# Cross-attention, block attention and a ternary feed-forward: value products ahead of the next scores, one quantization per slot

## The chip, the cores and the metric

The kernel runs on one core of one Trainium2 chip. The metric is the device time of one execution in microseconds. Three runs of the kernel before took 1119.99, 1122.01 and 1123.82 us; the median is 1122.01.

## The reference

`x` is 32 batches of 64 tokens of width 512, `ctx` is 32 batches of 1601 rows of width 512 with a mask. Three residual layers follow each other:

```python
x = x + xattn(layernorm(x), ctx, mask)   # 4 query heads of 128, one key/value head, rotary positions
x = x + attn(layernorm(x))               # 16 heads of 32, causal over the 64 tokens of a batch
x = x + ffn(layernorm(x))                # 512 -> 2048 -> 512

# attn
Q, K, V = heads(x @ WQ), heads(x @ WK), heads(x @ WV)
p = softmax(Q @ K.T / sqrt(32) + causal)
out = (p @ V) @ WO

# ffn: both weight matrices are made ternary in the kernel
gamma = mean(abs(W)) + 1e-6
Wq = sign(W / gamma) * minimum(round(abs(W / gamma)), 1)
h = layernorm(gelu(x @ Wq_fc.T)) * ln_w + ln_b
out = h @ Wq_proj.T
```

## The kernel before

All of it is one program with one instruction list per engine. A function at the head of the program looks at the mask and, when few context rows are valid, takes the path `few`, which is the one that runs here. Its stages are: cross-attention over 32 batches (0 to about 541 us), block attention over 16 blocks of 128 tokens, two batches each (about 541 to 835 us), and the feed-forward over the same 16 blocks (to the end).

The order of the work is written out by hand. `at(slot, order, fn)` enters a piece of work under a slot and an order number; `run_slots` then calls the pieces slot by slot and, within one, by order number. Each piece appends its instructions to the lists of its engines, so a smaller number means an earlier place on every engine that the piece uses. Each engine works through its list in order and stops at a wait. Waits are named by tokens (`tok[...]`). Slots are places in the order and have no fixed length.

Block attention begins at slot `B2`, and block i at `s = B2 + 4*i`. Below, slots are counted from `B2`. The even and the odd block of a pair share the projections (`s2_qk`, moving operand 256 columns), so the pattern repeats every eight slots:

- `s2_T` (order 5): transposes the layer-normed input of a block; ScalarE writes the high part of the split, VectorE the low part. `s2_qk` (4.1), one of eight groups a slot, for a later pair; each is 12 products (three terms of a split times four), evacuated by ScalarE. `s2_v` (4.4): the values, 12 products of 512 columns, and four small DMAs.
- `s2_scores` (order 1): 64 small matmuls into four PSUM banks; VectorE adds the causal mask (L930) and takes the maxima (L933), GpSimd subtracts them (L936).
- `s2_exp` (slot s+1): ScalarE, two halves b. `s2_PT` (s+2 and s+3, 2.7): four transposes each, evacuated by ScalarE (L949) for the value products.
- `s2_PV` (s+4, 4): the value products, 64 small matmuls; VectorE normalizes (L971 reciprocal, L974 product). This slot is also that of the scores of block i+1.
- `s2_ET` (s+5, 5.5): transposes of the normalized values and their split: high part on ScalarE (L230), low part on VectorE (L233). `s2_O` (s+6, 4.45): the output projection, 12 products of 512 columns, and `store`: VectorE adds the residual (L861), a DMA stores the rows.

Beside this run the 64 tiles of the feed-forward weights. `w_load(n)` loads tile n into one of four buffers; it is issued when tile n-4 is done with. For n below 32 `w_abs(n)` (3.9) sums absolute values on VectorE (L1008). Then `w_gamma` makes the scale: a small sum (L1015), one matmul with ones (L1018, the scale product), two small VectorE instructions. For n from 32, `w_quant(n)` (4.5) makes a ternary tile with two VectorE instructions (L1035, L1038) in one of two buffers, so it waits for the transposes of tile n-2. `w_T(n)` transposes it on TensorE (L1050, four bf16 matmuls, "ternary transposes" below), and ScalarE evacuates (L1059). In the kernel before `w_quant(n)` first calls `w_T(n - 1)`. Slots: tiles are spread evenly over 62 slots, from slot 1 to slot 62.

At the end of the stage the ternary weights are copied to float (`s3_WF`, L1125 on ScalarE, L1128 on VectorE, two each; slot 62, order 7.4, which waits for everything emitted until then), and the first feed-forward products `s3_h(0, n)` stand at slot 64 and following, order 1.5. The evacuation of the last block's second `s2_PT` (slot 63) stands behind these copies on ScalarE.

PSUM banks come from one list: a piece takes the bank that was given back longest ago.

Of the kernel before, what the change touches and what calls it, by code (L numbers as in the profile page):

```python
# [160 lines left out]
def few(nc, handle, bank, base, x1d, x2d, x, ctxd, mask, rms, qw, kvw, ow, WQ, WK, WV, WO, Wfc, lnw, lnb,  # L161
        Wproj, cosk, sink, cosq, sinq, identd, causald, out, picked, kmask, ktab, t_rows, nb=B):
    ni = nb // 2
# [237 lines left out]
    def at(slot, order, fn):  # L401
        count[0] += 1
        sched.setdefault(slot, []).append((order, count[0], fn))
# [273 lines left out]
    for b in range(nb):  # L677
# [22 lines left out]
        else:  # L700
            i = b // 2
# [20 lines left out]
    T0, B2 = FT * nb + 2, FT * nb + 24  # L722
# [216 lines left out]
    def s2_exp(i, b):  # L939
        tok["exp", i, b] = [op("act", lambda e: e.activation(  # L940
            sP[:, b, :, :], sP[:, b, :, :], ACT.Exp, scale=float(DK) ** -0.5), sem("a_exp"), [tok["nm", i, b]])]
# [11 lines left out]
    def s2_PV(i):  # L953

        ks = take(), take()
        free = [t for k in ks for t in gfree[k]]
        for b in range(2):
            for c in range(4):
                for x in range(2):
                    ps = slice(64 * x, 64 * x + 64)  # L960
                    for s in range(2):
                        m = (b * 4 + c) * 33
                        tk = products(bank[ks[x]][64 * s:64 * s + 64, m:m + 33],
                                      [(PT2[ps, b, c * 128 + 64 * s:c * 128 + 64 * s + 64],
                                        Vb[ps, i % 2, b, c, s, :])],
                                      "a_pv", [*tok["pt", i, 0], *tok["pt", i, 1], *tok["v", i], *free], check=True)
        tok["pv", i] = [tk]
        en = en2[:, :].rearrange("p (c b x f) -> p x b c f", c=4, b=2, x=2)
        for x in range(2):
            src = bank[ks[x]][:, 0:264].rearrange("p (b c f) -> p b c f", b=2, c=4)  # L970
            tr = op("dve", lambda e, x=x, src=src: e.reciprocal(rc2[:, x, :, :], src[:, :, :, 32]), sem("a_rc"),  # L971
                    [tk, *d2("en", i - 1)])
            rc = rc2[:, x, :, :].unsqueeze(3).to_broadcast([128, 2, 4, 32])
            t = op("dve", lambda e, x=x, src=src, rc=rc: e.tensor_tensor(en[:, x, :, :, :], src[:, :, :, 0:32], rc, ALU.mult),  # L974
                   sem("a_en"), [tr, *tok["late"], *d2("enT", i - 1)])
            give(ks[x], [t])
        tok["en", i] = [t]

    def s2_ET(i):
        k = take()  # L980
        dst = bank[k][:, :].rearrange("p (c r) -> p c r", c=4)
        tt = transposes(dst, [en2[:, c * 128:(c + 1) * 128] for c in range(4)], "a_enT",
                        [*tok["en", i], *gfree[k]])
        tok["enT", i] = [tt]
        tok["ET", i] = split("a_ET", dst, ET2[0][:, :, :], ET2[1][:, :, :], [tt, *tok["late"], *d2("o2", i - 1)])
        give(k, tok["ET", i])

    def s2_O(i):
        k = take()
        terms = []  # L990
        for c in range(4):
            terms += three(ET2[0][:, c, :], ET2[1][:, c, :], Wh[3][:, c, :], Wl[3][:, c, :])
        tk = products(bank[k][:, :], terms, "a_o", [*tW[3], *tok["ET", i], *gfree[k]])
        tok["o2", i] = [tk]
        store(i, x2d, k, tk)
# [11 lines left out]
    def w_abs(n):  # L1007
        ta = op("dve", lambda e: e.tensor_reduce(  # L1008
            asum[:, n // 16, n % 16:n % 16 + 1], wn[:, n % 4, :], AX.X, ALU.add,
            apply_absolute_value=True), sem("f_as"), [t_wn[n]])  # L1010
        wfree[n] = [ta]
        w_load(n + 4)
# [14 lines left out]
    def w_quant(n):  # L1027

        if n == 32:
            w_gamma()  # L1030
        else:
            w_T(n - 1)
        m = (n - 32) // 16
        w = wq_[:, n % 2, :]
        tq = op("dve", lambda e: e.tensor_scalar(w, wn[:, n % 4, :], gam[:, m:m + 1], -1.0,  # L1035
                                                 ALU.is_gt, ALU.add),
                sem("f_q"), [t_wn[n], *tok["gam"], *tok["late"], *tok.get(("wT", n - 2), [])])
        tq = op("dve", lambda e: e.scalar_tensor_tensor(  # L1038
            w, wn[:, n % 4, :], gam[:, 2 + m:3 + m], w, ALU.is_ge, ALU.add), sem("f_q"), [tq])
        wfree[n] = [tq]  # L1040
        if n + 4 < 64:
            w_load(n + 4)
        tok["wq", n] = [tq]

    def w_T(n):
        m, t = divmod(n - 32, 16)
        k = take()
        dst = bank[k][:, 0:256].bitcast(BF).rearrange("p (c r) -> p c r", c=4)
        for c in range(4):
            tt = op("pe", lambda e, c=c: e.transpose(dst[:, c, :], wq_[:, n % 2, c * 128:(c + 1) * 128],  # L1050
                                                     identb[:, :]),
                    sem("f_wT") if c == 3 else None,
                    [*tok["wq", n], t_idb, *gfree[k]] if c == 0 else ())
        tok["wT", n] = [tt]
        if m == 0:
            o = WFb[:, :, t * 128:(t + 1) * 128]
        else:
            o = WPb[:, (t % 4) * 4:(t % 4) * 4 + 4, (t // 4) * 128:(t // 4) * 128 + 128]
        tok["wb", m] = [op("act", lambda e: e.activation(o, dst, ACT.Copy), sem("f_W"),  # L1059
                           [tt, *tok["late"]])]  # L1060
        give(k, tok["wb", m])

    for i in range(ni):
        s, u, v = B2 + 4 * i, i // 2, i % 2
        o = B2 + 8 * u - 14 + 2 * v if u > 1 else (T0 - 7 + 2 * v if u == 0 else T0 + 4 + 2 * v)
        at(o - 1, 0, lambda i=i: ln_load(i))
        at(o, 3.4, lambda i=i: ln_stats(i))
        at(o + (1 if u > 1 else 3), 4.3, lambda i=i: ln_apply(i))
        at(B2 + 8 * u - 11 + v if u > 1 else T0 + 10 * u, 5, lambda i=i: s2_T(i))
        at(s - 1 if u else T0 + 10 + v, 4.4, lambda i=i: s2_v(i))  # L1070
        at(s, 1, lambda i=i: s2_scores(i))
        for b in range(2):
            at(s + 1, 3.0 + b, lambda i=i, b=b: s2_exp(i, b))
            at(s + 2 + b, 2.7, lambda i=i, b=b: s2_PT(i, b))
        at(s + 4, 4, lambda i=i: s2_PV(i))
        at(s + 4, 0, lambda i=i: res_load(i))
        at(s + 5, 5.5, lambda i=i: s2_ET(i))
        at(s + 6 if i else s + 8, 4.45, lambda i=i: s2_O(i))
    for u in range(ni // 2):
        for c in range(8):  # L1080
            at(B2 + 8 * u - 9 + c if u > 1 else T0 + 2 + c + 10 * u, 4.1 if u > 1 else 0.7,
# [15 lines left out]
    at(B2 + 3, 8.7, s2_outs)  # L1097
    at(B2 + 3, 8.8, lambda: s2_wload(3))
    for n in range(64):
        s = B2 - 2 + (n * (4 * ni - 2)) // 64  # L1100
        if n < 4:
            at(B2 - 1, 0.5, lambda n=n: w_load(n))
        if n < 32:
            at(s + 3, 3.9, lambda n=n: w_abs(n))
        else:
            at(s + 3, 4.5, lambda n=n: w_quant(n))
    B3 = B2 + 4 * ni
    at(B3 - 1, 9, lambda: w_T(63))

# [1269 lines left out]
```

How the kernel before makes its waits and increments, by code:

```python
    def op(self, eng, fn, sem=None, waits=(), inc=1):  # L47
        for w in waits:
            if w is None:
                continue
            s, v = w
            if self.seen[eng].get(s, 0) < v:
                self.seen[eng][s] = v
                self.q[eng].append(lambda e, s=s, v=v: e.wait_ge(s.h, v))
        if sem is None:
            self.q[eng].append(fn)
            return None
        self.q[eng].append(lambda e: fn(e).then_inc(sem.h, inc))
        sem.n += inc
        return (sem, sem.n)
# [7 lines left out]
        def f(e):  # L68
            with e.If(when()):
                for g in fns[:-1]:
                    g(e)
                fns[-1](e).then_inc(sem.h, 1)
            with e.Else():
                e.drain().then_inc(sem.h, 1)
# [267 lines left out]
        def g(e):  # L342
            with e.If(when()):
                f(e).then_inc(s.h, 16)
            with e.Else():
                e.sem_inc(s.h, 16)
# [1956 lines left out]
        def run(name, e):  # L2303
            early.play(name, e)
            first.play(name, e)
            fits = e.value_load(onepath[0:1, 0:1], min_val=0, max_val=1)
            with e.If(fits > 0):
                short.play(name, e)
            with e.Else():
                for s, n in [rows, *loaded[1]]:
                    e.wait_ge(s.h, n)
                long.play(name, e)
```

## Time and profile before

| what | value |
|---|---|
| median of three runs | 1122.01 us |
| profiled execution | 1122.38 us |
| its span | 1120.2 us |
| mean granted TensorE clock | 0.969 of full speed |
| TensorE busy | 956.8 us (85%) |
| VectorE busy | 688.4 us (61%) |
| ScalarE busy | 453.0 us (40%) |
| GpSimd busy | 441.0 us (39%) |
| mean of one L861, L1008, L1015 | 0.69, 0.67, 0.18 us |
| weight tile load, issue to landing (median) | 3.0 to 3.2 us |

TensorE busy times are modelled and overlap at the edges; a stop of TensorE is better read from the order of time, where a bracket gives the idle time in front of a group and the instruction that ended it. VectorE and ScalarE are half idle on the whole; what they do matters where TensorE stops for it. The granted clock has two levels, 1.2 and 2.4 GHz, shown as 0.5 and 1.0.

### The profile page before, as it was taken

How to read it: one execution, taken by the hardware profiler on the slowest of the kernel's cores; microseconds unless marked ns; L12 is line 12 of the kernel's file. 1: busy time of each engine (PE TensorE's matmuls, PEld its weight loads, DVE VectorE, ACT ScalarE, POOL GpSimd, SP SyncE). 2: the span in 40 equal slices, each digit the busy share in tenths (PEclk: the TensorE clock that was granted, in tenths of full speed). 3: DMA queues.
4: the chain of work that ended last, by engine and by line, in shares of the span. 5: the costliest groups of instructions: out<-in, count | busy, mean ns of one | idle time of the engine just before them, and what ended most of it. 6: DMA issues, size and time to landing. Idle time of an engine off the chain costs nothing.

```text
span 1120.2 us, 22904 instructions
## 1 busy us (share of the span) xinstructions
PE 956.8 (85%) x7466; PEld 809.4 (72%) x7466; DVE 688.4 (61%) x1352; ACT 453.0 (40%) x972; POOL 441.0 (39%) x572
## 2 busy tenths in 40 slices
PE   0898879888788888779798988889869999999996
PEld 0787757676676767668688887778647888888885
DVE  3587666766766767764545554655556665565554
ACT  2565445554455545444323232434363322322321
POOL 1354444444444444410212111111016767667663
PEclk9999999999999999979799998999879999999999
DMA  5532233221223222411534443334331111101101
GB/s 167 156 92 55 71 89 95 89 60 59 84 83 92 72 80 73 158 38 40 170 116 112 114 136 95 107 108 108 107 118 38 58 34 52 57 29 57 57 19 50
DMA packets 96769, 95.11 MB, mean 85 GB/s; under 512 B 41634, under 2 KB 58099, under 8 KB 96371
## 3 DMA queue, kind: packets, MB, share of 16 engines
q1 hardware_dynamic: 96016, 93.19, 28.3%
q8 instruction: 74, 1.21, 0.4%
q14 instruction: 69, 0.56, 0.2%
q10 hardware_dynamic: 578, 0.13, 0.1%
q0 software_dynamic: 32, 0.02, 0.0%
HBM read 76.45 MB, written 12.66 MB: 80 GB/s over the span
## 4 chain that ended last, share of the span: by engine, by line
PE 66%; DVE 15%; issue 10%; ACT 3%; DVEq 2%; ACTq 1%; POOL 1%; DMA 1%; SPq 0%; POOLq 0%
PE bank L244 52%; PE bank L219 9%; PE bank L240 4%; DVE f L233 3%; DVE f L507 2%; DVE f L930 2%; DVEq L74 1%; ACT f L230 1%; ACTq L74 1%; ACT f L412 1%; PE bank L529 1%; DVE f L974 1%; DVE f L470 1%; DMA f<-in_L_attn_WO_dram 1%; DVE f L641 1%
## 5 line engine op out<-in xcount | busy, mean ns | idle before, releaser
L244 PE MATMUL bank<-f,f 128*128 128x512 f32 (+3 forms) x5544 | 762.0, 312 | 62.4 <-issue 24.5
L244 PEld LDWEIGHTS bank<-f,f 128*128 128x128 f32 (+2 forms) x5544 | 596.5, 173 | 165.9 <-issue 67.6
L233 DVE TENSOR_TENSOR f<-bank,f 128x512 fp32r<-128x512 f32 x291 | 194.4, 686 | 129.9 <-ACT f L230 127.9
L219 PE MATMUL bank<-f,f 128*128 128x128 f32 x1152 | 170.3, 282 | 62.9 <-DVE f L619 28.7
L230 ACT ACTIVATE f<-bank 128x512 fp32r<-128x512 f32 x291 | 167.1, 593 | 110.3 <-PE bank L219 105.5
L219 PEld LDWEIGHTS bank<-f,f 128*128 128x128 f32 x1152 | 136.8, 145 | 90.1 <-DVE f L619 29.8
L936 POOL TENSOR_TENSOR f<-f,f 128x512 f32<-128x512 f32 x32 | 33.4, 1043 | 219.0 <-DVE f L933 219.0
L1153 ACT ACTIVATE f<-bank 128x512 f32<-128x512 f32 x64 | 38.3, 599 | 175.5 <-PE bank L244 175.5
L1176 POOL TENSOR_TENSOR f<-f,f 128x512 f32<-128x512 f32 x62 | 79.7, 1285 | 67.4 <-DVE f L1172 67.4
L468 POOL TENSOR_TENSOR f<-f,f 128x512 f32<-128x512 f32 x32 | 41.9, 1310 | 156.6 <-ACTq L74 135.2
L1178 POOL TENSOR_TENSOR f<-f,f 128x512 f32<-128x512 f32 x62 | 80.5, 1299 | 4.9
L261 POOL TENSOR_SCALAR f<-f 128x1 f32<-128x1 f32 (+1 forms) x112 | 22.9, 204 | 151.3 <-DVE f L840 84.5
L263 POOL TENSOR_TENSOR f<-f,f 128x1 f32<-128x1 f32 (+1 forms) x112 | 78.0, 697 | 9.3
L930 DVE TENSOR_TENSOR f<-bank,f 128x256 f32<-128x256 f32 x64 | 24.0, 418 | 72.5 <-PE bank L244 72.5
L518 ACT ACTIVATE f<-f,f 128x512 f32<-128x512 f32 x64 | 46.3, 724 | 50.4 <-DVE f L516 40.5
L884 ACT ACTIVATE f<-bank 128x256 f32<-128x256 f32 x64 | 24.4, 381 | 89.6 <-PE bank L244 89.6
L507 DVE CUSTOM_DVE_ANT_0 f<-bank,f 128x512 f32<-128x512 f32 x64 | 44.2, 690 | 25.3 <-PE bank L244 17.7
L240 PE MATMUL bank<-f,f 128*128 128x256 f32 x372 | 53.1, 290 | 7.5 <-issue 4.7
L240 PEld LDWEIGHTS bank<-f,f 128*128 128x128 f32 x372 | 46.6, 190 | 13.5 <-issue 13.3
L230 ACT ACTIVATE f<-f 128x256 fp32r<-128x256 f32 (+1 forms) x52 | 25.3, 497 | 70.8 <-DVE f L565 68.9
L861 DVE TENSOR_TENSOR f<-bank,f 128x512 f32<-128x512 f32 x32 | 22.1, 691 | 44.3 <-PE bank L244 44.3
L1172 DVE TENSOR_SCALAR f<-f,f,f 128x512 f32<-128x512 f32 x64 | 37.1, 580 | 16.4 <-POOL f L263 16.4
(88 smaller groups left out, 819.0 us busy)
## 6 DMA issues: line engine op xcount, KB each, us to landing
f<-in_ctx_dram SPq DMA_DIRECT2D x71, 256.0 KB, 2.8
f<-x_scratch SPq DMA_DIRECT2D x64, 256.0 KB, 3.0
f<-in_x_dram SPq DMA_DIRECT2D x32, 256.0 KB, 3.0
x_scratch<-f SPq DMA_DIRECT2D x32, 256.0 KB, 2.0
f<-in_L_ffn_W_fc_dram SPq DMA_DIRECT2D x32, 256.0 KB, 3.0
f<-in_L_ffn_W_proj_dram SPq DMA_DIRECT2D x32, 256.0 KB, 3.2
f<-in_ktab_dram SPq DMA_DIRECT2D x71, 64.0 KB, 2.0
f<-f SPq DMA_DIRECT2D x64, 64.0 KB, 2.4
```

The source lines that it names most:

```text
L219: f = lambda e, i=i, a=a: e.transpose(dst[:, i, :], a, ident[0:rows, 0:rows])
L230: return maybe("act", lambda e: e.activation(hi, src, ACT.Copy), sem(name + "_hi"), waits, when)
L233: return maybe("dve", lambda e: e.tensor_tensor(lo, src, hi.bitcast(F32), ALU.subtract), sem(name + "_lo"), waits, when)
L240: fns = [lambda e, i=i, a=a, b=b: e.matmul(dst, a, b, start=(first and i == 0), stop=(last and i == n - 1), skip_group_check=True) for i, ...
L244: f = lambda e, i=i, a=a, b=b: e.matmul(dst, a, b, start=(first and i == 0), stop=(last and i == n - 1), skip_group_check=check)
L263: return op("pool", lambda e: e.tensor_tensor(dst, tmp, mhalf[0:dst.shape[0], 0:n], ALU.pow), sem(name + "_p"), [t])
L468: ta = op("pool", lambda e: e.tensor_tensor(o1, K, cb, ALU.mult), sem("s_k1"), [tk, t_tab[b], *d("ktT", b - 2)])
L507: to = op("dve", lambda e: e.tensor_tensor_reduce(Pm[:, b % 2, t, :], bank[NL][:, :], bias[:, b % 2, :], 1.0, -3.0e38, ALU.add, ALU.max, m ...
L518: te = op("act", lambda e: e.activation(Pm[:, u, t, :], Pm[:, u, t, :], ACT.Exp, bias=nm[:, u, t:t + 1], accum_out=den[:, u, t:t + 1]), se ...
L930: f = lambda e, src=src, o=to[:, x, :, :]: e.tensor_tensor(o, src, cb, ALU.add)
L1176: t2 = op(eng, lambda e: e.tensor_tensor(g, g, lw[:, sl], ALU.mult), sem(f"f_y_{eng}"), [t1, tok["ln"]])
L1178: tok["y", i, n] = op(eng, lambda e: e.tensor_tensor(g, g, lb[:, sl], ALU.add), sem(f"f_y_{eng}"), [t2])
```

## The change

The value products of block i stand ahead of the scores of block i+1 in the same slot (order 0.5 instead of 4). Their output transposes stand at the end of that slot instead of the next (s+4, 5.5), and the output projection at the end of the slot after it (s+5, 5.6) instead of in slot s+6. The second half of the exponential stands at order 4.6 instead of 4.0. The absolute sums are spread over slots 1 to 26; quantization n follows with one tile a slot, in slots 27 to 58, at the beginning of its slot (0.3); `w_T(n)` is no longer called by `w_quant` but stands at order 4.5 of the slot after its quantization (28 to 59). No instruction is added or taken away.

```diff
@@ -1028,8 +1028,6 @@
 
         if n == 32:
             w_gamma()
-        else:
-            w_T(n - 1)
         m = (n - 32) // 16
         w = wq_[:, n % 2, :]
         tq = op("dve", lambda e: e.tensor_scalar(w, wn[:, n % 4, :], gam[:, m:m + 1], -1.0,
@@ -1070,12 +1068,12 @@
         at(s - 1 if u else T0 + 10 + v, 4.4, lambda i=i: s2_v(i))
         at(s, 1, lambda i=i: s2_scores(i))
         for b in range(2):
-            at(s + 1, 3.0 + b, lambda i=i, b=b: s2_exp(i, b))
+            at(s + 1, 3.0 + 1.6 * b, lambda i=i, b=b: s2_exp(i, b))
             at(s + 2 + b, 2.7, lambda i=i, b=b: s2_PT(i, b))
-        at(s + 4, 4, lambda i=i: s2_PV(i))
+        at(s + 4, 0.5, lambda i=i: s2_PV(i))
         at(s + 4, 0, lambda i=i: res_load(i))
-        at(s + 5, 5.5, lambda i=i: s2_ET(i))
-        at(s + 6 if i else s + 8, 4.45, lambda i=i: s2_O(i))
+        at(s + 4, 5.5, lambda i=i: s2_ET(i))
+        at(s + 5 if i else s + 7, 5.6, lambda i=i: s2_O(i))
     for u in range(ni // 2):
         for c in range(8):
             at(B2 + 8 * u - 9 + c if u > 1 else T0 + 2 + c + 10 * u, 4.1 if u > 1 else 0.7,
@@ -1097,15 +1095,15 @@
     at(B2 + 3, 8.7, s2_outs)
     at(B2 + 3, 8.8, lambda: s2_wload(3))
     for n in range(64):
-        s = B2 - 2 + (n * (4 * ni - 2)) // 64
+        s = B2 - 2 + (n * (4 * ni - 38) // 32 if n < 32 else 4 * ni - 70 + n)
         if n < 4:
             at(B2 - 1, 0.5, lambda n=n: w_load(n))
         if n < 32:
-            at(s + 3, 3.9, lambda n=n: w_abs(n))
+            at(s + 3, 0.3, lambda n=n: w_abs(n))
         else:
-            at(s + 3, 4.5, lambda n=n: w_quant(n))
+            at(s + 3, 0.3, lambda n=n: w_quant(n))
+            at(s + 4, 4.5, lambda n=n: w_T(n))
     B3 = B2 + 4 * ni
-    at(B3 - 1, 9, lambda: w_T(63))
```

## Rows read from the trace of the kernel before

**Rows 1.** Chain of waits of the whole execution, share of the span by engine.

```profile
PE 66%; DVE 15%; issue 10%; ACT 3%; DVEq 2%; ACTq 1%; POOL 1%; DMA 1%; SPq 0%; POOLq 0%
```

**Rows 2.** TensorE's waits from 540 to 840 us: total, times, longest.

```profile
PE bank L1050 <- DVE f L1038: 17.4, 9, 4.0
...
PE bank L244 <- DVE f L233: 8.8, 6, 2.2
...
PE bank L219 <- DVE f L974: 7.0, 6, 2.8
```

**Rows 3.** TensorE in order of time (start, length), part that quantizes; idle time in brackets.

```profile
714.04 4.41 PE L244 MATMUL bank<-f,f 128*128 128x256 f32 x24 [1.54 <-DVE f L233]
...
718.62 4.25 PE L244 MATMUL bank<-f,f 32*64 32x64 f32 x140
...
725.54 0.40 PE L1050 MATMUL bank<-f,f 128*128 128x128 bf16 x4 [0.95 <-DVE f L1038]
...
743.82 0.40 PE L1050 MATMUL bank<-f,f 128*128 128x128 bf16 x4 [1.75 <-DVE f L1038]
...
757.05 4.25 PE L244 MATMUL bank<-f,f 32*64 32x64 f32 x140
...
787.39 2.98 PE L244 MATMUL bank<-f,f 128*128 128x512 f32 x12
...
790.22 0.40 PE L1050 MATMUL bank<-f,f 128*128 128x128 bf16 x4
```

**Rows 4.** TensorE, part that only sums: two pair starts, and waits of 580 to 620.

```profile
616.35 10.06 PE L244 MATMUL bank<-f,f 128*128 128x256 f32 x176
...
651.45 8.74 PE L244 MATMUL bank<-f,f 128*128 128x256 f32 x165
...
PE bank L219 <- DVE f L974: 1.6, 2, 1.0
...
PE bank L244 <- DVE f L233: 1.2, 1, 1.2
```

**Rows 5.** TensorE in order of time, last two blocks and start of stage 3.

```profile
790.55 2.63 PE L244 MATMUL bank<-f,f 32*64 32x64 f32 x128
...
797.47 0.61 PE L1050 MATMUL bank<-f,f 128*128 128x128 bf16 x4 [3.96 <-DVE f L1038]
...
800.39 4.95 PE L244 MATMUL bank<-f,f 128*128 128x512 f32 x12 [0.61 <-issue]
...
808.95 2.63 PE L244 MATMUL bank<-f,f 32*64 32x64 f32 x128
...
830.37 7.43 PE L244 MATMUL bank<-f,f 128*128 128x512 f32 x80 [3.95 <-DVE f L1128]
```

**Rows 6.** VectorE in order of time behind one block's scores.

```profile
699.34 0.76 DVE L930 TENSOR_TENSOR f<-bank,f 128x256 f32<-128x256 f32 x2 [3.16 <-PE bank L244]
...
702.12 0.68 DVE L839 BATCH_NORM_STATS2 f<-f 128x6 f32<-128x512 f32 x1
...
702.94 0.19 DVE L971 RECIPROCAL f<-bank 128x8 f32<-128x8 f32 x1
...
704.07 0.48 DVE L1035 TENSOR_SCALAR f<-f,f 128x512 bf16<-128x512 f32 x1
```

**Rows 7.** TensorE around the scale product.

```profile
674.70 4.06 PEld L244 LDWEIGHTS bank<-f,f 32*64 32x64 f32 x140 [0.35 <-issue]
...
683.12 2.91 PE L244 MATMUL bank<-f,f 128*128 128x256 f32 x12
```

**Rows 8.** Window of one microsecond: busy time of PE, PEld, DVE, ACT, POOL; granted clock.

```profile
794.00:795.00 1.00, 0.00 (x0) 0.00 (x0) 0.97 (x3) 0.39 (x2) 0.82 (x1) 0.68 0.41 65
```

**Rows 9.** TensorE and ScalarE in the first pair.

```profile
548.84 3.46 PE L244 MATMUL bank<-f,f 32*64 32x64 f32 x128
...
548.95 0.60 ACT L949 ACTIVATE f<-bank 128x512 f32<-128x512 f32 x1 [0.72 <-PE bank L219]
...
561.59 14.37 PE L244 MATMUL bank<-f,f 128*128 128x256 f32 x188 [2.20 <-DVE f L233]
```

## The prediction

> **What bounds the kernel now.** I read the chain of waits first [rows 1]: TensorE carries two thirds of it, so the time falls only where TensorE stops. The change touches the second stage alone (541 to 835 us). There the list of TensorE's waits [rows 2] names what stops it: the ternary transposes waiting for the quantization (17.4 us), the next projection waiting for the low part of its input (8.8) and the output transposes waiting for the normalized values (7.0). Then I went through TensorE's order of time. One block of 128 tokens is four slots, two blocks share a projection; call slot 0 the first slot of stage 2. In the part that quantizes [rows 3] a pair of blocks takes 38.4 us (718.62 to 757.05), and three stops recur in it: 1.75, 0.95 and 1.54, together 4.25. In the part that only sums absolute values [rows 4] it takes 35.1 (616.35 to 651.45), with stops of 1.6 in two and 1.2, together 2.8. Without stops a pair costs 32.3, or 34.2 with eight ternary transposes.
>
> **The change part by part.** No instruction is added or removed; the sum is over stops, and over places where the clock falls.
>
> *Work per piece.* Score products take 1.25 us and value products as much (2.63 for both at full clock [rows 5]), a 512-column group 2.8 (787.39, next work at 790.22 [rows 3]), a projection group 1.5, four transposes 0.4, four ternary ones 0.25. On VectorE [rows 6] the mask additions and maxima of one block run from 699.34 to 702.12, 2.8; statistics to 702.94, 0.8; normalization to 704.07, 1.15; one quantization 1.2. Masks start 0.5 after the last score product.
>
> *Quantization and its transposes.* Quantization n now stands at the head of a slot, its transposes near the end of the next. It waits for the transposes of n-2 (the slot before, TensorE's last item there), so it starts about 0.15 into the slot and ends at 1.35. Behind it on VectorE is the normalization, which cannot start before the value products end (1.25) plus 0.5 = 1.75. So it hides, with 0.4 to spare, and a whole slot later nothing waits for it: the stops of 1.75 and 0.95 go. If that cover were gone, each such block pays up to 1.2 - 0.4 = 0.8.
>
> *Value products ahead of the scores.* The normalization then runs 1.75 to 2.9, beside the scores (1.25 to 2.5); masks follow at 3.0 (0.5 after the scores), where they would have started anyway. The output transposes come after scores, one projection group and the ternary transposes, at 4.3: no stop, so the 1.6 go too.
>
> *Output projection a slot sooner.* This costs. Its input's low part is a VectorE subtraction emitted at the end of the slot of the scores, behind masks (3.0 to 5.8) and, in every second block, the statistics (to 6.6). With 0.65 for itself and 0.15 to be seen, the projection can start at 6.6 or 7.4. TensorE arrives at 4.3 + 0.4 + 1.5 + 0.25 = 6.45 (6.8 with one input transpose between): stops of 0.15 and 0.6; without ternary transposes it is there 0.5 sooner, so 0.65 and 1.1. Before, a slot more hid this. The stop of the next projection stays, 1.54 falling to 1.2 (its subtraction no longer stands behind a quantization).
>
> Per pair: 34.2 + 0.15 + 0.6 + 1.2 = 36.15 with quantization, against 38.4: -2.3. Without it 32.3 + 0.65 + 1.1 + 1.2 = 35.2, against 35.1: +0.1.
>
> *Stretch by stretch.* Slots 8 to 24: two pairs, +0.2. Slots 24 to 32: four of the ternary transposes move in here (+1.1), stops 0.65 + 0.6 + 1.15 for 2.8 (-0.4), and the scale's product, now at slot 27. It follows on VectorE the output addition (0.7), the last sum (0.65), statistics (0.8) and a small sum (0.2), seen 2.8 after the projection's end, while TensorE arrives after 0.4 + 1.5: 1.0 and its own 0.3. Together +2.0. Slots 32 to 40: before, the pair with the scale product took 718.62 - 674.70 = 43.9, as TensorE stood before it and after it, then ran at half clock, 1.2 of 2.4 GHz (2.91 for 12 matmuls of 256 columns [rows 7]); I take 43.7, since the first mark is a weight load. Now an ordinary 36.1: -7.6. Slots 40 to 48: -2.3. Slots 48 to 56 (33.5; no input transposes or statistics): 2 x 0.95 go, 2 x 0.15 come, -1.6.
>
> *Slots 56 to 60, no projections left* [rows 5]. Before: 808.95 - 790.55 = 18.4, with a stop of 3.96 and a half-clock output projection of 4.95. Now: values and scores to 2.5, ternary 2.8, output transposes at 3.05 (normalization) to 3.45, ternary to 3.7; then the projection waits for masks (5.8), its subtraction (6.45): start 6.65, a stop of 3.0. Does the clock fall in it? It fell at 794.4 (a mean of 0.68 from 794 to 795 is 0.36 us at full clock [rows 8]), less than 1 us after TensorE's last work, and not in stops of 1.75 [rows 3]. 3.0 is nearer to 3.96 than to 1.75; I take the fall: 4.8 for the projection, to 11.45, then 0.4 + 0.25 + 0.4 + 2.85 + 0.25 to 15.6. -2.8 (warm -4.8; both ends kept).
>
> *From slot 60 to the third stage.* Before: 21.4 from 808.95 to the first product of stage 3 at 830.37, which waited for a weight conversion, itself behind the store of the projection before. Now the projection (behind masks, statistics, subtraction) starts at 7.45 and is cold, ends 12.4; three sets of transposes to 14.6; store and semaphores let the conversions on ScalarE start at 16 to 17 (2.65 after the store's issue, as before), two take 3.7, and only then comes the evacuation that the value products need, as these now stand ahead of the first product of stage 3: 20.6 to 21.7. They run 1.7 cold, then the product 3.4 cold: 25.7 to 26.8 for work that ended before at 26.6. -0.4, between -2 and +2. What leaves these slots (the four last quantizations) gains nothing more, since the chain store, conversion, evacuation ends last.
>
> *The start, slots 0 to 8* [rows 9]. Now the first value products wait for the copy of the second set of transposes (548.95 + 0.60, seen at 549.7), 0.85 after TensorE is free, and the scores behind them come 1.7 late at half clock (3.46 for both). Masks shift by 2.75, less 1.15 for the normalization now ahead of them; the input's subtraction, which holds the first projection at 561.59, lies behind all that: +1.6, a little less by ScalarE. I take +1.5, between -0.5 and +3.
>
> The exponential's new place (behind one more projection copy) costs nothing: its transposes are a slot and a half away. Weight loads are issued four sums or quantizations ahead, three slots at least, some 13 us (35.1 / 8 x 3 [rows 4]) before use, and land in about 3: nothing. Store and residual load move with the projection; the residual lands before the addition in every stretch. Bounds of all these: 0 to +1.
>
> Sum: 1.5 + 0.2 + 2.0 - 7.6 - 2.3 - 1.6 - 2.8 - 0.4 = -11.0. The profiled execution took 1122.38 (span 1120.2 and 2.2 around it), 0.4 above the median of the three runs (1122.01). 1122.4 - 11.0 = **1111.4 us**.
>
> **The rivals.** *A, the forecast.* 55%, own range 1107 to 1117.
>
> *B, the low part is no stop and the clock holds.* If VectorE reaches the subtraction before TensorE gets to the projection, the stops that I charge go: 2 x 1.75 in slots 8 to 24, 1.25 in 24 to 32, 2 x 0.75, 0.3: 6.5; and a clock that holds in slots 56 to 60 gives 2.0 more. 1109.4 with the clock alone, 1103 with both. For it: the merged VectorE rows hide overlaps of up to 0.1 per instruction. Against: the order of emission is plain. 22%. On the clock, the Trainium skill (TensorE: Matmul & The Clock Gate, What's actually happening) lets the monitor run on its own time and not from the program's start, so equal gaps may end differently; the fall after a short stand [rows 8] agrees. By that rule 1109.4 would be about as likely as 1111.4.
>
> *C, the quantization holds up the normalization.* It starts only when TensorE has done the transposes of n-2; if that is seen 0.4 later than I reckon, normalization, masks and subtraction slip in the nine blocks of slots 28 to 60, by up to 0.8: +7.5, 1118.9, no change. For it: the wait was a slot away before and is now next door. Against: 0.4 of room. 14%.
>
> *D, slower: the stop at the output projection lets the clock fall.* Place: slot 5 of each pair. If masks and subtraction come 0.9 later than reckoned, the stop of 1.1 becomes 2.0, and TensorE falls to half clock as after the scale product, where a projection group took 2.91 for 1.5 [rows 7]. Price: 0.9 x 14 blocks = 12.6, and two such groups, 2.8, in each of the three pairs of slots 8 to 32: 8.4. 1111.4 + 21 = 1132. Without a fall the delay alone must reach (11.0 + 3.4) / 14 = 1.0 per block to end slower. For it: the stop is new and recurs, and a second one of 1.2 follows some 5 us later. Against: stops of 1.75 recur without a fall [rows 3]. 9%.
>
> **How the numbers follow.** About 0.3% (3.4 us) is what a measurement of this kernel can tell from no change. A and B are faster: 0.77; C is same: 0.14; D slower: 0.09. The range takes in most of B and C: 1103 to 1120.
>
> **What would show it.** Right: waits of the ternary transposes for the quantization near zero, no wait of output transposes for the normalization, a pair with quantization near 36.1, the scale product costing 1 to 1.5 with no half clock behind it; and a new wait of TensorE for the split's subtraction just ahead of the output projection, 0.15 to 1.1, then 3 in slot 57 and 4 in slot 61. Wrong: ternary transposes still waiting (C), granted clock under 1.0 in slots 8 to 56 (D), or a first product of stage 3 that starts as late after slot 60 as before while its value products are still to come.

## The result and the profile after

The changed kernel takes **1112.41 us** (median of 5 runs, 1107.35 to 1112.48) against 1122.01 of the kernel before: a ratio of 0.990, interval 0.987 to 0.993. Forecast were 1111.4 and "faster".

The stretches are read from the starts of the value evacuations (L900), one in each block, from the first score product (541.45 us before, 544.18 after), and from the first full group of 16 products of stage 3 (856.62 before, 846.61 after).

| slots | before | after | difference | forecast |
|---|---|---|---|---|
| 0 to 8 | 26.1 | 27.1 | +0.95 | +1.5 |
| 8 to 24 | 72.1 | 72.1 | 0.0 | +0.2 |
| 24 to 32 | 35.1 | 35.9 | +0.8 | +2.0 |
| 32 to 40 | 43.7 | 35.9 | -7.8 | -7.6 |
| 40 to 48 | 38.4 | 35.7 | -2.7 | -2.3 |
| 48 to 56 | 33.5 | 31.6 | -1.9 | -1.6 |
| 56 to 60 | 18.4 | 15.2 | -3.2 | -2.8 |
| 60 to stage 3 | 47.8 | 48.9 | +1.1 | -0.4 |
| rest | 263.6 | 263.6 | 0.0 | 0 |
| first score product to end | 578.7 | 566.0 | **-12.7** | -11.0 |

Below, "first score to end" is this last row, for every kernel, from its profiled execution. It ends with a piece that no edit touches, from the last addition to the end of the span, 6.96 to 8.39 us in the twelve kernels; differences of about 1 us can lie there alone. The span shrank by only 10.0: stage 1, which is the same code, was 2.7 longer in this execution. TensorE's busy time and mean granted clock between 150 and 165 us, first after, then before (columns: window, its length, PE busy, clock, DMA share, GB/s):

```profile
150.00:165.00 15.00, 12.25 (x58) 0.81 0.39 124
```

```profile
150.00:165.00 15.00, 11.92 (x69) 1.00 0.44 132
```

The clock fell there in one execution and not in the other. So the forecast's total is nearer to the median (1.0) than its stage-2 sum is to the measured one (1.7), and that is luck.

TensorE's waits in stage 2 after (total, times, longest), to be set beside [rows 2]:

```profile
PE bank L244 <- DVE f L233: 11.5, 10, 2.8
PE bank L244 <- ACT f L949: 8.1, 2, 7.4
PE bank L244 <- issue: 6.3, 6, 3.8
...
PE bank L1018 <- DVE f L1015: 0.4, 1, 0.4
PE bank L219 <- DVE f L974: 0.3, 1, 0.3
```

The ternary transposes (17.4 before) are gone from the list, the normalization (7.0) nearly so. New are the waits of the output projection for the low part of its input, part of L233 and all of "issue" (in each of the six places the subtraction ends 0.1 before the projection starts), and 7.4 of the last value products behind L949. The chain of waits [rows 1] breaks off after a quarter of the span, at a load in stage 3 that GpSimd waits for; that load comes up again below.

TensorE in order of time after, the part that only sums [rows 4]:

```profile
580.57 3.04 PE L244 MATMUL bank<-f,f 128*128 128x512 f32 x12 [0.49 <-DVE f L233]
...
597.40 3.04 PE L244 MATMUL bank<-f,f 128*128 128x512 f32 x12 [0.79 <-issue]
...
604.26 8.61 PE L244 MATMUL bank<-f,f 128*128 128x256 f32 x164 [1.07 <-DVE f L233]
...
615.23 3.04 PE L244 MATMUL bank<-f,f 128*128 128x512 f32 x12 [0.49 <-DVE f L233]
```

The 512-column groups are the output projections: stops of 0.49 and 0.79 (forecast 0.65 and 1.1), then 1.07 for the next pair's input. A pair takes 34.66 (580.57 to 615.23; forecast 35.2, before 35.10). The pair in front of it, which still holds the start of the stage, takes 37.5 for 37.0, so slots 8 to 24 come out even. The part that quantizes [rows 3]:

```profile
703.26 3.03 PE L244 MATMUL bank<-f,f 128*128 128x512 f32 x12 [0.33 <-issue]
...
710.69 4.42 PE L244 MATMUL bank<-f,f 128*128 128x256 f32 x24 [1.41 <-DVE f L233]
...
715.28 4.25 PE L244 MATMUL bank<-f,f 64*64 64x33 f32 x140
...
751.01 4.25 PE L244 MATMUL bank<-f,f 64*64 64x33 f32 x140
```

A pair takes 35.73 (715.28 to 751.01; forecast 36.15, before 38.4), with 0.33 and 1.41 left of 4.25. VectorE at the head of a slot with scores [rows 6]:

```profile
715.98 0.75 DVE L1036 SCALAR_TENSOR_TENSOR f<-f,f,f 128x512 bf16<-128x512 f32 x1
716.93 0.21 DVE L971 RECIPROCAL f<-bank 128x8 f32<-128x8 f32 x1 [0.20 <-PE bank L244]
```

The normalization waits 0.20 for the value products, not for the quantization ahead of it. The scale product now stops TensorE for 0.4, and the projection behind it runs at full clock, where [rows 7] show 2.91 for 12 matmuls (here 24 in 4.42):

```profile
655.18 0.38 PE L1018 MATMUL bank<-f,f 128*128 128x2 f32 x2 [0.41 <-DVE f L1015]
...
655.81 4.42 PE L244 MATMUL bank<-f,f 128*128 128x256 f32 x24
```

The last two blocks [rows 5], TensorE and then ScalarE:

```profile
782.63 2.64 PE L244 MATMUL bank<-f,f 64*64 64x33 f32 x128
...
789.25 4.30 PE L244 MATMUL bank<-f,f 128*128 128x512 f32 x12 [2.79 <-DVE f L233]
...
797.85 2.64 PE L244 MATMUL bank<-f,f 64*64 64x33 f32 x128
...
805.21 5.46 PE L244 MATMUL bank<-f,f 128*128 128x512 f32 x12 [3.76 <-issue]
...
819.65 5.46 PE L244 MATMUL bank<-f,f 64*64 64x33 f32 x72 [7.40 <-ACT f L949]
```

```profile
815.35 3.71 ACT L1123 ACTIVATE f<-f 128x2048 fp32r<-128x2048 bf16 x2 [2.85 <-DMA f<-x_scratch]
818.97 0.58 ACT L949 ACTIVATE f<-bank 128x512 f32<-128x512 f32 x1
```

Stops of 2.79 and 3.76 (forecast 3 and about 4). Then the two conversions, 3.71, with the evacuation of the probabilities behind them, and TensorE idle 7.40 for it. The clock in slot 57 (columns: window, its length, busy time of PE, PEld, DVE, ACT, POOL, clock, DMA share, GB/s):

```profile
790.00:791.00 1.00, 1.00 (x5) 0.78 (x4) 0.70 (x1) 0.29 (x1) 0.00 (x0) 0.81 0.00 0
791.00:792.00 1.00, 1.00 (x3) 0.79 (x3) 0.00 (x0) 0.00 (x0) 0.00 (x0) 0.50 0.00 0
```

It fell at about 790.6 (0.81 of that microsecond), more than 1 us after TensorE was at work again, and was back at 794.

### The profile page after: what moved, and what is told of

Same layout as the page of the kernel before. It is cut to its first block and busy times, and to the rows that moved or that the text cites. A ratio compares the mean times of both kernels' runs of the same rounds, so it can differ in the third digit from the quotient of the medians.

```text
span 1110.2 us, 22910 instructions
## 1 busy us (share of the span) xinstructions
PE 956.3 (86%) x7466; PEld 809.7 (73%) x7466; DVE 693.2 (62%) x1352; ACT 452.8 (41%) x972; POOL 443.4 (40%) x572
## 5 line engine op out<-in xcount | busy, mean ns | idle before, releaser
L233 DVE TENSOR_TENSOR f<-bank,f 128x512 fp32r<-128x512 f32 x291 | 194.5, 685 | 128.8 <-ACT f L230 126.8
L230 ACT ACTIVATE f<-bank 128x512 fp32r<-128x512 f32 x291 | 167.4, 593 | 112.7 <-PE bank L219 107.5
L263 POOL TENSOR_TENSOR f<-f,f 128x1 f32<-128x1 f32 (+1 forms) x112 | 79.8, 713 | 9.3
L507 DVE CUSTOM_DVE_ANT_0 f<-bank,f 128x512 f32<-128x512 f32 x64 | 44.2, 690 | 25.7 <-PE bank L244 18.4
L230 ACT ACTIVATE f<-f 128x256 fp32r<-128x256 f32 (+1 forms) x52 | 25.3, 496 | 69.4 <-DVE f L565 69.0
L412 ACT ACTIVATE f<-f 128x512 bf16<-128x512 f32 x71 | 44.0, 620 | 3.2 <-ACT f L412 2.2
```

What stands on the lines that cost most here:

```text
L230: return maybe("act", lambda e: e.activation(hi, src, ACT.Copy), sem(name + "_hi"), waits, when)
L233: return maybe("dve", lambda e: e.tensor_tensor(lo, src, hi.bitcast(F32), ALU.subtract), sem(name + "_lo"), waits, when)
L263: return op("pool", lambda e: e.tensor_tensor(dst, tmp, mhalf[0:dst.shape[0], 0:n], ALU.pow), sem(name + "_p"), [t])
L412: done["sq"] = maybe("act", lambda e: e.activation(sq[:, :], cx[:, b % NG, t, :], ACT.Square, accum_out=ss[:, b % 4, t:t + 1]), sem("s_ss" ...
L507: to = op("dve", lambda e: e.tensor_tensor_reduce(Pm[:, b % 2, t, :], bank[NL][:, :], bias[:, b % 2, :], 1.0, -3.0e38, ALU.add, ALU.max, m ...
```

## The experiments

Experiments 1 to 4, 5 to 8, and 9 and 10 ran on one chip each, beside the kernel before.

### 1. The weights' half of the change alone

The kernel after with the attention's lines as before, all edits on sums, quantizations and ternary transposes kept:

```
-            at(s + 1, 3.0 + 1.6 * b, lambda i=i, b=b: s2_exp(i, b))
+            at(s + 1, 3.0 + b, lambda i=i, b=b: s2_exp(i, b))
...
-        at(s + 4, 0.5, lambda i=i: s2_PV(i))
+        at(s + 4, 4, lambda i=i: s2_PV(i))
-        at(s + 4, 5.5, lambda i=i: s2_ET(i))
-        at(s + 5 if i else s + 7, 5.6, lambda i=i: s2_O(i))
+        at(s + 5, 5.5, lambda i=i: s2_ET(i))
+        at(s + 6 if i else s + 8, 4.45, lambda i=i: s2_O(i))
```

> Only the weight part of the change: absolute sums in slots 1 to 26, one quantization at the head of a slot, transposes a slot later; value products, output transposes, output projection and exponential stand as before. Measured from the first score product of stage 2 to the end of the span: 578.7 us before, 566.0 with the whole change. Theory (the gain is the weight part's: scale product and its half clock, ternary transposes that no longer wait; moving the attention pieces brings stops of its own): about 560, 556 to 564, so more gain than the whole change; no wait of TensorE for the quantization, waits of the output transposes for the normalization of 0.4 at most, none of the output projection for the subtraction. Rival (the value products ahead of the scores bring the gain): 572 to 577.

Measured: 1105.39 us (1103.84 to 1106.52), 0.984 of before (0.982 to 0.987); first score to end 563.6, 2.4 below the whole change. Slots 32 to 40 take 35.8, as after. That is 3.6 above the theory's 560 and far from the rival: all of the gain, and more, comes from the weights' half. Of the theory's signs, no ternary transpose waits for its quantization. The output projection does wait for the subtraction, 0.35 in three places, and the normalization stops TensorE for 0.41 in the part that sums but for 2.2 to 3.1 in the first pair and the last two blocks. Slots 8 to 24 take 70.3 for 72.1 with no edit on the attention: there only the place of the sums differs.

### 2. The attention's half alone

The kernel before with those lines of the kernel after.

> Only the attention part: value products ahead of the next scores, output transposes and projection sooner, second exponential later; the weights are summed, quantized and transposed in their old places. First score product to the end: theory 577 to 583 (no gain: the scale product keeps its stop and half clock, the ternary transposes still wait, now for a quantization behind masks, and the output projection waits for a subtraction behind that quantization); rival 566 to 572.

Measured: 1133.22 us (1130.2 to 1136.19), 1.009 of before (1.006 to 1.013); first score to end 589.7. Neither theory went so far up. TensorE in the part that sums:

```profile
578.63 3.04 PE L244 MATMUL bank<-f,f 128*128 128x512 f32 x12 [1.09 <-DVE f L233]
...
596.05 3.04 PE L244 MATMUL bank<-f,f 128*128 128x512 f32 x12 [1.38 <-issue]
```

The same two stops as after, each 0.6 longer: the sums stand in their old place (3.9), one of them (0.7 on VectorE) ahead of the subtraction that the projection needs. That is 2.3 of the loss of 11.0, in slots 8 to 24. Slots 48 to 56 lose 3.4 and the way to stage 3 3.0. In slot 49 the clock falls at the output projection, and 20 us later, behind stops of the same length (1.40 before the ternary transposes, then 0.25), it does not:

```profile
769.96 4.58 PE L244 MATMUL bank<-f,f 128*128 128x512 f32 x12 [0.25 <-issue]
...
789.85 3.04 PE L244 MATMUL bank<-f,f 128*128 128x512 f32 x12 [0.25 <-issue]
```

### 3. The change with the output projection in its old slot

```
-        at(s + 5 if i else s + 7, 5.6, lambda i=i: s2_O(i))
+        at(s + 6 if i else s + 8, 4.45, lambda i=i: s2_O(i))
```

> The whole change, but the output projection back in its old place (a slot later). First score product to the end, 566.0 with the change: theory 562 (the stops of 0.5, 0.8 and 0.3 ahead of the projections in slots 8 to 56 go, 4 us in all, and no stop takes their place; the last blocks are about even). Rival (the earlier projection pays at the end of the stage, where its store is waited for): 567 to 570.

Measured: 1102.31 us (1101.69 to 1105.31), 0.982 of before (0.979 to 0.985); first score to end 559.3. TensorE in the part that sums has no stop at the output projections, and those of the normalization (L974) stay away too:

```profile
599.41 8.62 PE L244 MATMUL bank<-f,f 128*128 128x256 f32 x164 [1.07 <-DVE f L233]
...
610.09 0.66 PE L219 MATMUL bank<-f,f 128*128 128x128 f32 x4 [0.20 <-ACT f L940]
```

That is 2.7 better than the theory. Slots 8 to 24 take 69.0 (72.1 after). The sooner output projection costs 6.7 us (7.7 up to the last addition); the other attention moves gain 4.3 (563.6 to 559.3; 3.9 up to the last addition). In the change the one ate up the other.

### 4. The weight conversions for stage 3 a slot sooner

They wait for the last value projection alone and stand in the third slot from the end:

```
-    at(B3 - 2, 7, lambda: mark("qkv_end"))
+    at(B3 - 3, 5.2, lambda: tok.update(qkv_end=tok["proj", ni // 2 - 1]))
     for n in range(4):
-        at(B3 - 2, 7.4, lambda n=n: s3_WF(n))
+        at(B3 - 3, 5.3, lambda n=n: s3_WF(n))
```

> The whole change, and the copies of the first feed-forward weights to float a slot earlier and waiting only for the last value projection, whose weights they overwrite, not for everything emitted (the store of a projection among it). First score product to the end, 566.0 with the change: theory 557.5 (the stop of 7.4 ahead of the last value products falls to about 1, and TensorE's clock does not fall in it, some 2 us more). Rival (the copies on VectorE and ScalarE now delay the split of the last blocks, and the time is given back ahead of the output projection): 562 to 565.

Measured: 1106.68 us (1104.04 to 1108.16), 0.985 of before (0.982 to 0.988); first score to end 564.7, the rival's number. From slot 60 to stage 3 it takes 46.5 for 48.9; the last piece behind the last addition is 0.9 longer here. TensorE at the last value products, then ScalarE a little later:

```profile
810.29 3.28 PE L244 MATMUL bank<-f,f 64*64 64x33 f32 x72 [0.84 <-ACT f L949]
...
818.24 6.41 PE L244 MATMUL bank<-f,f 128*128 128x512 f32 x20 [2.38 <-DVE f L233]
```

```profile
814.99 1.28 ACT L1151 ACT_TABLE_LOAD   x1 [3.00 <-issue]
...
816.78 0.59 ACT L230 ACTIVATE f<-bank 128x512 fp32r<-128x512 f32 x1
```

The stop of 7.40 is down to 0.84. But the last split (L230) now stands behind the first activation of stage 3 and its table load, and TensorE waits 2.38 there, still at half clock. A wait taken away, and the next one met.

### 5. The sums and the scale product sooner, nothing else

The kernel before with the sums in slots 1 to 26 and the scale product in slot 27:

```
...
-        s = B2 - 2 + (n * (4 * ni - 2)) // 64
+        s = B2 - 2 + (n * (4 * ni - 38) // 32 if n < 32 else (n * (4 * ni - 2)) // 64)
...
+    at(B2 + 27, 0.3, w_gamma)
```

> The kernel before, with one part of the change alone: the absolute sums in slots 1 to 26 and the scale product in slot 27; quantization, transposes and attention stay where they were. Measured from the first score product to the end of the span (578.8 us before, 566.0 after, 563.6 with all edits on the weights). Theory: the 7.8 us that slots 32 to 40 lost come from the scale product leaving a place where TensorE stood 1.6 us before it and then ran at half clock; slots 32 to 40 take 38.4 like slots 40 to 48 before, slots 24 to 32 1 more: 573 to 576. Rival: the stop and the half clock go along with the product, and the gain was the quantization's: 577 to 580.

Measured: 1123.77 us (1119.87 to 1127.21), 1.001 of before (0.999 to 1.003); first score to end 578.8. The theory fails: slots 32 to 40 take 41.2, only 2.5 less. The total is the rival's, its reason is not: slots 24 to 32 take 35.9, as after, so the stop and the half clock did not go along with the product. TensorE in slots 32 to 40:

```profile
684.80 0.61 PE L1048 MATMUL bank<-f,f 128*128 128x128 bf16 x4 [2.67 <-DVE f L1036]
685.16 2.83 PE L244 MATMUL bank<-f,f 128*128 128x256 f32 x12
```

The scale product no longer stands there, but the first ternary transposes still wait for their quantization, 2.67, and behind them 12 matmuls take 2.83 again: half clock.

### 6. The quantizations at the head of their slot, nothing else

The kernel before with this (transposes where they were; the two first tiles unchanged):

```
...
-            at(s + 3, 4.5, lambda n=n: w_quant(n))
+            at(s + 3, 0.3 if n > 33 else 4.5, lambda n=n: w_quant(n))
+            if n > 32:
+                at(s + 3, 4.5, lambda n=n: w_T(n - 1))
```

> The kernel before, with another part alone: the quantizations from n = 34 at the head of their slot (0.3) and not at 4.5; the transposes stay where they are, and so do the sums, the scale product and the attention. Theory: the head of the slot is what takes away the stop of the ternary transposes (17.4 us in nine before); slots 40 to 48 35.8 (38.4 before), 48 to 56 31.6 (33.5), 56 to 60 17.5 (18.4), slot 60 to the third stage 2 less, and a part of it in slots 32 to 40: first score product to end 567 to 571 (578.8 before). Rival: a quantization at the head holds up masks and normalization as long as the value products stand behind the scores, so that the stop only moves to the output transposes: 575 to 579.

Measured: 1115.16 us (1113.71 to 1118.49), 0.994 of before (0.992 to 0.995); first score to end 573.6. Slots 40 to 48 take 35.8, 48 to 56 31.6, 56 to 60 17.1: as the theory says. Slots 32 to 40 lose 1.6 only, and the way to stage 3 does not shrink (48.4 for 47.8). The rival has a share in the last two blocks: there the output transposes wait 2.55 each for the normalization. Where the scale product stands, TensorE shows:

```profile
677.78 0.38 PE L1018 MATMUL bank<-f,f 128*128 128x2 f32 x2 [1.57 <-DVE f L1015]
...
680.00 0.61 PE L1048 MATMUL bank<-f,f 128*128 128x128 bf16 x4 [1.84 <-DVE f L1036]
680.37 2.91 PE L244 MATMUL bank<-f,f 128*128 128x256 f32 x12
```

So slots 32 to 40 lose 2.5 by one part, 1.6 by the other and 7.9 by both (experiment 1). Experiment 5 keeps a stop of 2.67, experiment 6 two of 1.57 and 1.84 close together, and in both the clock falls; in experiment 1, with neither, it is 1.00 throughout these slots.

### 7. The ternary transposes in the slot of their quantization

```
-            at(s + 4, 4.5, lambda n=n: w_T(n))
+            at(s + 3, 4.5, lambda n=n: w_T(n))
```

> The changed kernel, with the ternary transposes at the end of the slot of their quantization (slots 27 to 58), not of the next. Theory: from its head a quantization is done 1.4 us into the slot and TensorE comes to the transposes some 4 us into it, so nothing waits; the slot between is not needed: first score product to end 565 to 567 (566.0 after). Rival: the quantization waits for the transposes of tile n-2 and stands behind other VectorE work, so that the transposes wait again by 1 us or more in each of 32 slots: over 575.

Measured: 1130.41 us (1128.0 to 1133.31), 1.006 of before (1.004 to 1.008); first score to end 586.0. The rival holds, though not in each of the 32 slots: nine of the ternary transposes wait, 19.6 us in all, nearly all of them right behind a slot with scores. TensorE, and VectorE in the same slots:

```profile
709.76 0.40 PE L1048 MATMUL bank<-f,f 128*128 128x128 bf16 x4 [2.15 <-DVE f L1036]
...
710.61 4.36 PE L244 MATMUL bank<-f,f 128*128 128x512 f32 x12
```

```profile
704.27 0.76 DVE L930 TENSOR_TENSOR f<-bank,f 128x256 f32<-128x256 f32 x2
...
707.86 0.66 DVE L233 TENSOR_TENSOR f<-bank,f 128x512 fp32r<-128x512 f32 x1
708.44 0.48 DVE L1033 TENSOR_SCALAR f<-f,f 128x512 bf16<-128x512 f32 x1
708.95 0.75 DVE L1036 SCALAR_TENSOR_TENSOR f<-f,f,f 128x512 bf16<-128x512 f32 x1
```

This quantization heads its slot in the program, but VectorE still has the masks, statistics and subtraction of the slot before, 704.27 to 708.4. TensorE, which had begun the slot at 705.9, arrives at the transposes at 707.6. Where the slot before held scores and statistics, the head of a slot on VectorE comes 2.5 us into it.

### 8. Three edits to the change

Experiments 3 and 4 together, and the value projection of each even block ahead of the next pair's first key projection:

```
-        at(s - 1 if u else T0 + 10 + v, 4.4, lambda i=i: s2_v(i))
+        at(s - 1 if u else T0 + 10 + v, 4.4 if v or not u else 4.05, lambda i=i: s2_v(i))
```

> The changed kernel with three edits: the output projection back in its old slot (559.3 from the first score product to the end, when done alone), the weight conversions for the third stage released a slot sooner (564.7 alone, 1.3 less than after), and the value projection of each even block ahead of the first key projection of the next pair in the same slot, so that the low part of the input has one projection (2.8 us) more time. Theory: the stop of 1.07 before the key projection goes, six times, 1.2 more with the quantizations: 559.3 - 1.3 - 6.5 = 551.5, 549 to 554. Rival: the stop only moves (to the scores behind, or to the input transposes that come later on ScalarE): 556 to 560.

Measured: **1092.21 us** (1090.15 to 1093.6), 0.972 of before (0.969 to 0.975); first score to end 549.5, inside the theory's range. TensorE's waits in stage 2 (four of under 1 left out):

```profile
PE bank L219 <- DVE f L846: 12.3, 4, 4.9
PE bank L219 <- ACT f L940: 8.5, 6, 3.7
PE bank L244 <- ACT f L949: 1.5, 2, 0.7
```

The subtraction (L233; 11.5 after) stops TensorE nowhere. Experiment 3 still had these stops at the key projection (7.0 in six), so the third edit takes them; it was not run alone. Nearly all that is left lies in the first pair and behind slot 56.

### 9. The first block's value products behind the scores again

An edit of experiment 8's kernel:

```
-        at(s + 4, 0.5, lambda i=i: s2_PV(i))
+        at(s + 4, 0.5 if i else 4, lambda i=i: s2_PV(i))
```

> The kernel with three edits (549.5 us from the first score product to the end), and the value products of the very first block behind the scores again, as in the kernel before; all others stay ahead. Theory: the first value products stand 3.7 us behind the copy of the probabilities and hold up the scores behind them, which is the loss of 0.95 that slots 0 to 8 show; without it those slots are 1 shorter (22.5 for 23.5 in this arrangement), the total 548 to 549. Rival: the start is held by VectorE and ScalarE behind the first scores in either order, and nothing changes: 549.2 to 550.

Measured: 1089.87 us (1088.47 to 1096.17), 0.973 of before there (0.969 to 0.978), with experiment 8's interval inside it: no difference. First score to end is 548.7, which is the theory's number, but not from its place: slots 0 to 8 take 23.5 in both. TensorE:

```profile
545.60 3.46 PE L244 MATMUL bank<-f,f 32*64 32x64 f32 x128
552.28 1.97 PE L219 MATMUL bank<-f,f 128*128 128x128 f32 x8 [3.22 <-DVE f L974]
```

Scores and value products start sooner (7.4 after the first score product for 8.2), and then TensorE stands 3.22 for the normalization. The rival holds, in this arrangement. What costs slots 0 to 8 their 0.95 in the change is one of the attention's moves other than the output projection: experiment 1 without them is 0.4 under the kernel before there, experiments 2, 3 and 10 are 0.8 to 1.3 over it. Which one is left open.

### 10. The attention's half without the output projection

The kernel before with the value products, the exponential and the output transposes moved, the output projection not.

> The kernel before with the attention's moves, except the output projection, which stays in its old slot; sums, quantizations and transposes in their old places. With the output projection moved as well, this took 589.7 us from the first score product to the end (578.8 before). Theory: only the output projection's move costs (stops of 1.09 and 1.38 in each pair, for 0.99 and 0.64 that go), the others gain with any arrangement of the weights: slots 8 to 24 69 to 70 (72.1 before, 74.5 with the projection moved), the total 570 to 575. Rival: with the quantizations in their old place every attention move lengthens VectorE's queue ahead of the transposes, and the loss stays: 583 to 588.

Measured: 1121.58 us (1118.2 to 1124.0), 1.000 of before (0.998 to 1.002); first score to end 576.5, between the two. Slots 8 to 24 take 68.9, as the theory says. In the part that quantizes the rival has a share: 40 to 48 and 48 to 56 take 0.4 and 1.0 more than before, and the ternary transposes wait more, not less (17.4 before):

```profile
PE bank L1050 <- DVE f L1038: 19.5, 9, 4.2
```

## Why the prediction was right, and where not

**Quantization and its transposes: right in size, wrong in one reason.** The stops of 1.75 and 0.95 went, and the pair came to 35.7 (forecast 36.15). But the step has it start "about 0.15 into the slot" and end at 1.35. That holds in the slots with scores (679.39 to 679.57). In the slots right behind them it starts 1.7 or 2.5 into the slot (684.08 to 685.78, 700.58 to 703.07), and without a slot between, the transposes wait again (experiment 7). So the head of the slot is not enough; the slot between is needed too. The kernel before had that, with the quantization at 4.5, and it was not enough either. With sums and scale product left alone the new place brings 5.2 (experiment 6).

**Slots 32 to 40: the size right, the cause half right.** The step goes from 43.7 to an ordinary pair of 36.1. That is 5.3 for the scale product and its half clock (43.7 to 38.4) and 2.3 for the quantization. Alone the one brings 2.5 there, and nothing over the whole stage (experiment 5), the other 1.6 (experiment 6): each leaves stops behind which the clock falls. The forecast came out since the change removes both.

**Value products ahead, output projection sooner: right.** The stops at the output projection were 0.49 and 0.79 for 0.65 and 1.1, and 0 and 0.33 for 0.15 and 0.6. VectorE was as reckoned: the subtractions ended 6.47 and 7.27 after the value products of their blocks began (679.39 to 685.86, 695.89 to 703.16) for 6.45 and 7.25; TensorE came up to 0.24 later than the 6.45 and 6.8 put down. The smaller stops make a pair that only sums 0.5 shorter than forecast. Rival B puts the stops charged to this move at 6.5 in all, and undoing it brings 6.7 (experiment 3). So the price was known; what the sum by stretches did not show is that the other attention moves gain only 4.3, and that leaving this one out would have been better.

**Slots 0 to 8: +1.5 forecast, +0.95 measured.** The first value products came 0.8 later for 0.85, the masks behind them 2.67 for 2.75. The way from these masks to the first projection then took 1.8 less, where the step has 1.15.

**Slots 24 to 32: +2.0 forecast, +0.8 measured.** The scale product's stop was mis-sized: 0.41 for 1.0. It came 2.4 after the end of the output projection (652.75 to 655.18) for 2.8, and TensorE's own work up to there took 2.0 for 1.9. (2.8 less 1.9 is 0.9, not 1.0.) The other half of the difference is in the three other stops, 2.05 for 2.4, and in smaller pieces.

**Slots 56 to 60: right.** A stop of 2.79 for 3.0. The clock did fall, but behind the stop and not in it, so the projection took 4.30 for 4.8 (3.0 at full clock, 5.46 at half in slot 61).

**Slot 60 to stage 3: +1.1 for -0.4, inside its bounds.** The value products started 21.8 after slot 60 (797.85 to 819.65) for 20.6 to 21.7, behind the conversions as described. Of the products from there on, the first 132 ended 41.9 after slot 60 (839.77), before 41.8 (850.77): +0.1. The missing 0.9 is a wait that the step does not have, of the next transposes for GpSimd's part of stage 3's normalization, here after and then before:

```profile
841.45 0.65 PE L219 MATMUL bank<-f,f 128*128 128x128 f32 x4 [1.68 <-POOL f L1176]
```

```profile
851.51 0.66 PE L219 MATMUL bank<-f,f 128*128 128x128 f32 x4 [0.74 <-POOL f L1178]
```

GpSimd itself waits after, and not before, for a load of that normalization's parameters:

```profile
838.77 1.29 POOL L1174 TENSOR_TENSOR f<-f,f 128x512 f32<-128x512 f32 x1 [1.39 <-DMA f<-in_L_ffn_ln_b_dram]
```

The load stands in SyncE's list behind the store of the last output projection once that projection is a slot sooner: it is issued 0.9 us behind that store in the kernel after, and 12 us ahead of it in the kernel before. All four kernels with the sooner output projection show the longer wait (1.66 to 1.81), all eight others 0.73 or 0.74. So this too is a cost of the output projection's move, which the prediction has only in its bounds for store and residual load (0 to +1).

**The total.** Seven terms came out 0.2 to 1.2 better than forecast and the last 1.5 worse, and stage 1 was 2.7 longer in the profiled execution. That the total is only 1.0 off is in part luck.

**The rivals.** C did not happen: the normalization waits for TensorE, not for the quantization (and nine times 0.8 is 7.2, not 7.5). B happened in part: smaller stops, and a clock that fell late in slot 57. D did not happen: the granted clock is 1.00 from 571 to 782. Experiment 2 shows how near it was: with one sum more ahead of the subtraction the stops are 1.09 and 1.38, and the clock falls at one output projection (4.58 in slot 49). The Trainium skill (TensorE: Matmul & The Clock Gate, What's actually happening) has the monitor run on its own time, and experiments 2 and 7 agree: in 7, of equal stops of 2.15, the one ending at 670.02 left the next 512-column group at 3.05 us, the one ending at 709.76 at 4.36.

## What to carry to other kernels

Place work of a second engine by where that engine stands when the first gets there, not by the slot's name: behind a slot of scores, "the head of the slot" was up to 2.5 us late. Try each part of a bundle of moves by itself: here one part cost 6.7 us, unseen in a total that fell, and two parts of 2.5 and 1.6 made 7.9 together in the same eight slots, as each alone left stops behind which the clock fell. When a piece with a store moves, see what stands behind that store in the list of the engine that issues it. An operand in two parts is ready only with its second part; a projection put ahead of the one that needs it took those stops away entirely.

## What the runs showed of the hardware that had not been expected

Stage 1 is the same code in all twelve kernels, and its end, the first score product, lay between 538.2 and 545.1 us; the windows above show a clock fall in one execution and none in the other, and the first fall there (granted clock 0.73 from 148 to 150) came behind a stop of 1.53 us that the other execution has too (1.52, clock 1.00). That scatter is 0.6% of the kernel, and differences of one stage are better read from a mark inside the execution than from the whole time. The far end scatters too: from the last addition to the end of the span it takes 6.96 before, 7.03 after, and up to 8.39 (experiment 1).

A 128x1 power on GpSimd (L263) takes 0.55 us beside a sum on VectorE. It takes 1.06 in the three places where it lies beside the second instruction of a quantization, which reads two tiles (692.25 and 728.15 after, 817.15 before), and 0.71 in three where only its end lies beside it. VectorE then waits for it, 0.45 for 0.38. No run tries this by itself.
